# Attention with a low-rank feed-forward term: where the projection groups of the later batches stand among scores and sums

## What is computed

```python
    x = L0_attn_x                                  # (8, 1024, 256)
    xn = _layernorm(x, axis=-1)
    q = xn @ wq.T + bq;  k = xn @ wk.T + bk;  v = xn @ wv.T + bv
    attn = softmax(q @ k.T * 256 ** -0.5)
    lilora_weight = up_aux @ (lora_up @ (lora_down @ down_aux))
    return x + attn @ v + xn @ W.T + b + xn @ lilora_weight.T
```

## Time and profile before

| | us |
|---|---|
| median of 3 runs | 533.85 (533.81 to 533.9) |
| profiled execution, its own time | 533.79 |
| its span | 532.0 |
| TensorE busy (3734 matmuls) | 519.8, 98% |
| weight loads | 489.4, 92% |
| VectorE busy | 433.2, 81% |
| GpSimd busy | 335.3, 63% |
| ScalarE busy | 287.2, 54% |

### The profile page before, as it was taken

How to read it: one execution, slowest core, us unless ns; L and a number is a source line. 1 busy time by engine, 2 the same in 40 slices (tenths; PEclk the granted TensorE clock), 3 DMA queues, 4 the chain that set the end, 5 groups by cost and what they waited for, 6 DMA issues and landing times.

```text
span 532.0 us, 10118 instructions
## 1 busy us (share of the span) xinstructions
PE 519.8 (98%) x3734; PEld 489.4 (92%) x3734; DVE 433.2 (81%) x1162; ACT 287.2 (54%) x749; POOL 335.3 (63%) x205
## 2 busy tenths in 40 slices
PE   5999999999999999999999999999999999999996
PEld 4689999999999999999999999999999999999996
DVE  3679888978988788977988788988889777777896
ACT  2656666257474466564663565724657546344442
POOL 2813853989548975689548895489854895433330
PEclk9999999999999999999999999999999999999999
DMA  8020113002210023000330030200300000000001
GB/s 240 30 80 1 34 73 93 22 21 100 64 43 15 22 99 100 22 21 9 90 101 21 20 99 27 76 20 22 100 21 22 20 2 21 22 20 21 21 3 58
DMA packets 10933, 25.17 MB, mean 47 GB/s; under 512 B 2337, under 2 KB 3973, under 8 KB 9989
## 3 DMA queue, kind: packets, MB, share of 16 engines
q1 hardware_dynamic: 9344, 24.38, 13.6%
q10 hardware_dynamic: 1540, 0.16, 0.2%
HBM read 16.15 MB, written 8.39 MB: 46 GB/s over the span
## 4 chain that ended last, share of the span: by engine, by line
PE 86%; DVE 8%; DMA 2%; ACT 1%; issue 1%; SPq 0%; POOL 0%; DVEq 0%; POOLq 0%
PE s_ps L895 11%; PE s_ps L897 11%; PE s_ps L896 11%; PE o_ps L983 10%; PE o_ps L979 10%; PE o_ps L981 10%; PE g_ps L895 8%; PE g_ps L897 8%; PE g_ps L896 8%; DVE s L761 2%; DMA x_sb<-in_L_attn_x 2%; DVE tile_max L727 1%; ACT x_t L523 1%; DVE p_lo L773 1%; DVE xt_lo L684 0%
## 5 line engine op out<-in xcount | busy, mean ns | idle before, releaser
L467 POOL TENSOR_TENSOR p_lo<-s,p_hi 128x1024 fp32r<-128x1024 f32 x62 | 149.5, 2411 | 163.9 <-ACT p_hi L589 143.5
L581 ACT ACTIVATE s<-s,e 128x256 f32<-128x256 f32 x256 | 109.5, 499 | 128.2 <-DVE s L761 128.0
L979 PE MATMUL o_ps<-v_hi,p_hi 128*128 128x258 f32 x512 | 144.8, 283 | 1.3 <-DVE p_lo L773 1.0
L983 PE MATMUL o_ps<-v_hi,p_lo 128*128 128x258 f32 x512 | 144.7, 283 | 0.0
L981 PE MATMUL o_ps<-v_lo,p_hi 128*128 128x256 f32 x512 | 144.3, 282 | 0.0
L895 PE MATMUL s_ps<-xt_hi,zt_hi 128*128 128x256 f32 x504 | 143.1, 284 | 0.0
L897 PE MATMUL s_ps<-xt_hi,zt_lo 128*128 128x256 f32 x504 | 142.4, 283 | 0.0
L896 PE MATMUL s_ps<-xt_lo,zt_hi 128*128 128x256 f32 x504 | 142.3, 282 | 0.0
L727 DVE SCALAR_TENSOR_TENSOR tile_max<-s_ps,e,tile_max 128x256 f32<-128x256 f32 x221 | 106.7, 483 | 21.7 <-PE s_ps L897 12.9
L979 PEld LDWEIGHTS o_ps<-v_hi,p_hi 128*128 128x128 f32 x512 | 96.7, 189 | 4.0 <-DVE p_lo L773 1.4
L895 PEld LDWEIGHTS s_ps<-xt_hi,zt_hi 128*128 128x128 f32 x504 | 96.2, 191 | 3.1 <-DVE zt_lo L689 0.4
(11 more groups left out here) (134 smaller groups left out, 756.7 us busy)
## 6 DMA issues: line engine op xcount, KB each, us to landing
out<-base SPq DMA_DIRECT2D x31, 256.0 KB, 2.5
x_sb<-in_L_attn_x SPq DMA_DIRECT2D x7, 1024.0 KB, 5.7
x_t<-in_x_t SPq DMA_DIRECT2D x6, 1024.0 KB, 5.9
x_sb<-in_L_attn_x SPq DMA_DIRECT2D x4, 256.0 KB, 6.7
s<-in_L_attn_wk SPq DMA_DIRECT2D x1, 256.0 KB, 3.1
s<-in_L_attn_wq SPq DMA_DIRECT2D x1, 256.0 KB, 6.2
s<-in_L_attn_wv SPq DMA_DIRECT2D x1, 256.0 KB, 7.1
s<-in_L_ffn_W SPq DMA_DIRECT2D x1, 256.0 KB, 8.2
```

The source lines that it names most:

```text
L467: nc.gpsimd.tensor_tensor(p_lo[g % 2][:, keys, :], s[:, keys, :], p_hi[g % 2][:, keys, :].bitcast(f32), ALU.subtract)\
L581: nc.scalar.activation(s[:, n, :], s[:, n, :], ACT.Exp, bias=e[b % 2][:, n:n + 1])\
L979: nc.tensor.matmul(o_ps[u][:, 0:D + ONES], p_hi[g % 2][:, n, q], v_hi[i][:, n, :], start=(n == 0), stop=False)
L983: mm = nc.tensor.matmul(o_ps[u][:, 0:D + ONES], p_lo[g % 2][:, n, q], v_hi[i][:, n, :], start=False, stop=(n == TILES - 1))
```

## The change

The table holds tuples, and the loops go over all groups of a place. The new rows put the groups of chunks 1 to 3 at places 2 and 3 only; chunk 0 stays as it was.

```diff
-        LATER = [{2: 4, 3: 5}, {0: 6, 2: 7, 3: 8}, {0: 9, 2: 10, 3: 11}, {0: 12, 1: 13, 2: 14, 3: 15}]
-
-        def group_at(b, c, place):
+        LATER = [{2: (4,), 3: (5,)}, {2: (6, 7), 3: (8,)}, {2: (9, 10), 3: (11,)}, {2: (12, 13), 3: (14, 15)}]
+
+        def groups_at(b, c, place):
             if b + 1 == B:
-                return None
-            return PLACES * c + place if b + 1 < EARLY else LATER[c].get(place)
+                return ()
+            return (PLACES * c + place,) if b + 1 < EARLY else LATER[c].get(place, ())
@@ the same in make_group_hi_at, make_group_lo_at and group_of_next
-                if group_at(b, c, place) is not None:
-                    group(b + 1, group_at(b, c, place))
+                for k in groups_at(b, c, place):
+                    group(b + 1, k)
```

More of the change, by code:

```diff
@@ L540, in make_group_hi_at @@
             def make_group_hi_at(b, c, place):
-                if group_at(b, c, place) is not None:
-                    make_group_hi(b + 1, group_at(b, c, place))
+                for k in groups_at(b, c, place):
+                    make_group_hi(b + 1, k)
             def make_e_sum(b, tiles):
@@ L701, in make_group_lo_at @@
             def make_group_lo_at(b, c, place):
-                if group_at(b, c, place) is not None:
-                    make_group_lo(b + 1, group_at(b, c, place))
+                for k in groups_at(b, c, place):
+                    make_group_lo(b + 1, k)
             def make_stat_rows(b):
```

## The result

| | before | after |
|---|---|---|
| median, us | 533.83 (4 runs, 533.19 to 533.9) | 597.75 (4 runs, 595.32 to 600.33) |
| profiled run, us | 533.79 | 595.32 |
| its span | 532.0 | 593.5 |
| mean granted clock | 1.00 | 0.968 |

The change makes the kernel slower: ratio 1.1201, 95% interval 1.1152 to 1.125. The prediction was 579.5 us with a range up to 590. The direction is right and the time is outside the range, 18.3 us above the forecast.

A forecast was written before the change was run, and what follows sets the result against it. TensorE was taken to bound the kernel from 62 to 500 us. Its new waits at place 3, 16.6 + 18.1 + 6.8 + 4.2 = 45.7 us, added to 533.8, gave 579.5 us, with an 8 in 10 range of 576 to 590.

The forecast's parts named there:

- What bounds the kernel: From 62 to 500 us TensorE has no waits to give back; every us it loses is a us of the kernel.
- Steps 2 to 5: TensorE's place 3 waits: chunks 1, 2, 3 of batches 1 to 5 cost 16.6, 18.1, 6.8 us; batch 6 costs 4.2.
- step 2: Chunk 1, batches 1 to 5: place 3 waits 3.32 us for VectorE's lo part of place 2, 16.6 us in all.
- Step 1: Whole kernel: no instruction added or removed, six matmuls of a group take 1.40 us at any place; cost 0.
- step 7: Beside the waits: freed VectorE time, lone scores and p_lo make nothing late; taken as 0, with 0 to +12 us kept.
- the part on the clock: TensorE's matmul pace behind new waits up to 3.6 us: no run shows a fall, so without it the sum stands.
- the sum of 45.7 us: Waits at place 3 in chunks 1 to 3, batches 1 to 6: 16.6 + 18.1 + 6.8 + 4.2 us.
- Rival A: Clock falls after ten long waits, chunks 1 and 2, batches 1 to 5: 31 us more, 611; a few, 583 to 595; chance 0.10.
- One of the prediction's signs: In the changed kernel's profile, TensorE's busy time stays at 520 us.
- Rival B: VectorE or GpSimd falls behind and the next chunk's sums start late: up to +12 us, 583 to 592; chance 0.05.
- Rival C: VectorE does statistics and transposes before the sums' end; 18 waits of 1.36 us remain, 24.5 us, 558 us; chance 0.05.
- Rival D: Lo part of group 6, 9 or 12 done when TensorE asks: no waits, 533.2 to 533.8 us; chance 0.02.

The follow-up runs named there:

- The second experiment: Changed kernel with VectorE taking out place 2's groups right behind the output step, statistics and transposes behind them; 557.85 us, ratio 1.045.

## Why the prediction was wrong

Right, by its own steps:
- What bounds the kernel. Every us of TensorE's waiting was a us of the kernel, as the earlier trace rows said: 557.85 and 579.34 us are 533.8 plus the waits.
- Steps 2 to 5. The three kinds of wait were forecast as 3.32, 3.62 and 1.36 us and measure, from the due start to the usual pace again, 3.32, 3.61 and 1.35; batch 6 has the short kind in all three chunks (in its chunk 1 1.35 for the 1.45 forecast). VectorE's rows of before, laid against T, were the rows of after, because VectorE stood waiting at the sums' end in both. That waiting was shorter than step 2 had it where the scores first stand alone (in chunk 1 of batch 3 the shifts end at T - 1.12 and not at T - 2.0, and the reciprocal has 0.96 us of idle time before it), but long enough. The restart of the earlier trace rows, 0.06 and 0.11, was the same at every wait behind which the clock was still up.
- Step 1 (moving work costs nothing) and step 7 (nothing beside is late in the changed kernel): the kernel with the old table and the added wait has the same waits and the same time as the changed one.

Wrong: the part on the clock. The step that failed is the sum of 45.7 us, which put the cost of a falling clock at nothing; the term measures 15.7 us in the profiled run and 18.4 in the medians. Rival A had the mechanism and got a chance of 0.10; it was the case. As the reason against it I wrote that each wait is followed by 17 us without a gap; what follows does not matter, since the slow stretch begins at the restart or up to 1.4 us behind it, and in three cases of the changed kernel the clock fell within the wait, before that work can count. The trace of before had no wait longer than 0.6 us behind the start, so it could not speak against a fall after 3.6 us, and I let its silence count as evidence. The rule of the Trainium skill (TensorE: Matmul & The Clock Gate, "HAM oscillation — how this bites in real kernels") had said that waits between bursts bring the half clock each time. Here nearly each time: 9 of 10, with the granted clock of 0.50 in the stretches above.

The price in rival A was too high in one factor: I took 3.1 us a fall from the slow stretch at the program's start, where matmuls of other kinds and gaps stand among it. A stretch costs 1.4 to 1.6, sometimes 2.7 us, since it is over after 3.2 to 3.5 us (or about 6) and loses some 44% of that (starts 0.21 apart instead of 0.12). With the right price, nine or ten falls give the measured time and not 611 us; the milder part of the rival, 583 to 595, ended right below the measured 595.3 to 600.3.

One of the prediction's signs did not fit its own sum: TensorE's busy time was to stay at 520 us, though 45.7 us of waits with only 41 of them idle lengthen it by some 5. The second experiment, without slow stretches, has 523.8; the changed kernel has 541.1.

Rival B (the next chunk late): did not occur, there is no new wait before o_ps L979. Rival C, as it stood, was run: 557.85 against its 558. Rival D claimed that another order on VectorE alone would be enough for no loss. It wasn't: 540.3 us, because the hi part was not there in time. In step 2 I let it end at T - 0.9 and took VectorE as idle from T - 2.0. The changed kernel's row shows 1.83 us of idle time in chunk 2. Where the scores first stand alone, the shifts end at T - 1.1 in both kernels, which would have been time enough for a lo part of 0.72; but ScalarE's hi part is ready only at about T, and the lo part then makes TensorE 0.80 late.

## What to carry to other kernels

When two uses of a double buffer move together, ask what the emptying engine's queue holds between them: here a bank that was emptied among other work came to stand behind a wait for the very work that TensorE does before it asks. Read the wait's length from the rows of that queue, laid against the moment of the asking; that was exact to 0.01 us for the two long kinds and to 0.1 for the others. And give any new idle time of TensorE of 2 us or more a second term for the clock: here it was 1.4 to 2.8 us for each fall, and the table above has how often one came. Where such a wait cannot be removed, matmuls of no use in it can save that term.

## What the runs showed of the hardware

- The clock falls after idle times as short as 2 us, not each time, and the oftener the longer the wait: the table above. The slow stretch begins with the first matmul of the restart or up to 1.4 us behind it; it lasts 3.2 to 3.5 us. Where the granted clock fell 0.8 to 0.9 us before the restart (0.66 in the wait's last us above), seven times over all profiled runs, it lasts 5.9 to 6.1; where it fell only about 0.1 us before it, twice, the usual 3.4. What decides between falling and not at a given length was not settled.
- The time at half clock differs between executions of one kernel, and the kernel's time with it: 595.3 us at a mean granted clock of 0.968 and 600.3 at 0.957 for the changed kernel, 595.9 to 599.7 with the added wait, against 533.2 to 534.2 and 557.4 to 557.9 for kernels without falls.
- Matmuls of no use while waiting were worth 18.4 us: 579.34 against 597.75 us.
- At the program's start 256-column matmuls are 0.21 apart as well, but the granted clock reads 1.00 there; after the first fall the row reads 0.50 for the same pace. The prediction named for this, which begin at 62 us; a stretch of the changed kernel's start shows it (busy and matmuls of PE, PEld, DVE, ACT, POOL, then the granted clock):

```profile
11.00:12.00 1.00, 1.00 (x5) 1.00 (x6) 0.62 (x3) 0.27 (x1) 0.56 (x2) 1.00 1.16 395
```

For the start, the distance of the matmuls is the better sign of the clock.
